# Second attention of a fused kernel: stacked f16 scores, projections spread between scores, unnormalized transposes, a swap by DMA

## What is computed

```python
q, k = rope(q, k)          # q*cos + rotate_half(q)*sin, likewise k
scores = einsum('bhqd,bhkd->bhqk', q, k) / sqrt(32)
tmp_attn = softmax(scores + causal)
tmp_sum = sum(tmp_attn, axis=-2)
topk_idx = top_k(tmp_sum, 25)        # "heavy" columns, per head
mask = heavy_mask | (abs(i - j) <= 25)
probs = softmax(where(mask, scores, lowest))
x = x + (einsum('bhqk,bhkd->bhqd', probs, v) -> (b, s, 512)) @ Wo.T
```

## Time and profile before

| | |
|---|---|
| median of 3 runs | 2003.69 us (2002.29 to 2006.08) |
| the profiled execution's own time | 2005.3 us |
| its span in the trace | 2003.5 us |
| TensorE (PE) busy | 1884.2 us, 94% of the span |
| VectorE (DVE), ScalarE (ACT), GpSimd (POOL) busy | 1347.1, 980.5, 127.0 us |
| second attention's first scores to next stage's first product | 72.88 to 719.71 us |

### The profile page before, as it was taken

How to read it: one execution, slowest core, us unless ns; L and a number is a source line. 1 busy time by engine, 2 the same in 40 slices (tenths; PEclk the granted TensorE clock), 3 DMA queues, 4 the chain that set the end, 5 groups by cost and what they waited for, 6 DMA issues and landing times.

```text
span 2003.5 us, 80904 instructions
## 1 busy us (share of the span) xinstructions
PE 1884.2 (94%) x34632; PEld 1646.3 (82%) x34632; DVE 1347.1 (67%) x5146; ACT 980.5 (49%) x3438; POOL 127.0 (6%) x213
## 2 busy tenths in 40 slices
PE   5899999899998889998899999999999999999998
PEld 3676776776777669998799899899998998998988
DVE  4476866767677665555767766767767777667664
ACT  2344653455435555665444554544554554545443
POOL 1120120210202101111000000000000000000000
PEclk9999999999999899999999999999999999999999
DMA  7011010110102113433000000100101000000000
GB/s 279 31 46 45 1 46 1 46 46 1 46 17 93 64 32 97 144 124 123 4 19 19 14 19 19 30 4 19 30 4 30 20 19 14 19 19 14 4 13 12
DMA packets 55611, 81.59 MB, mean 41 GB/s; under 512 B 5641, under 2 KB 42377, under 8 KB 54737
## 3 DMA queue, kind: packets, MB, share of 16 engines
q1 hardware_dynamic: 50960, 64.84, 9.7%
q0 software_dynamic: 4288, 11.55, 1.9%
HBM read 61.13 MB, written 15.24 MB: 38 GB/s over the span
## 4 chain that ended last, share of the span: by engine, by line
PE 53%; DVE 6%; ACT 2%; issue 1%; DMA 1%; DVEq 0%; ACTq 0%; POOLq 0%
PE ps L1348 27%; PE ps L1302 11%; PE ps L1281 10%; PE ps L1269 5%; DVE dh L1565 1%; ACT nn L1422 1%; DVE dh L1571 1%; DVE hn L1558 1%; DVE nxt L1574 0%; PE ps L1335 0%; DVE nxt L1577 0%; DVE tn L1540 0%; PE ps L1249 0%; DVE rn L1552 0%; DMA shared<-in_w2T 0%
## 5 line engine op out<-in xcount | busy, mean ns | idle before, releaser
L1348 PEld LDWEIGHTS ps<-nxt,whp 128*128 128x128 f16 x24576 | 649.2, 96 | 46.6 <-DVE nxt L1577 38.9
L1348 PE MATMUL ps<-nxt,whp 128*128 128x32 f16 x24576 | 655.8, 176 | 29.4 <-DVE nxt L1577 26.9
L1422 ACT ACTIVATE rz<-s,sc 128x32 f32<-128x32 f32 x512 | 164.8, 322 | 450.1 <-DVE s L1540 449.8
L1281 PE MATMUL ps<-cur,w1p 128*128 128x256 f16 x2112 | 271.8, 274 | 0.2 <-DVE wip L1716 0.2
L1302 PE MATMUL ps<-shared 128*128 128x256 f16 x2112 | 265.8, 273 | 0.0
L1302 PEld LDWEIGHTS ps<-shared 128*128 128x128 f16 x2112 | 205.6, 98 | 23.6
L1540 DVE TENSOR_REDUCE s<-ps 128x32 f32<-128x64 f32 x512 | 114.9, 224 | 162.5 <-PE ps L1348 161.6
L1281 PEld LDWEIGHTS ps<-cur,w1p 128*128 128x128 f16 x2112 | 198.3, 98 | 22.6 <-DVE wip L1716 0.4
L543 PE MATMUL ps<-kz,rot 128*128 128x256 f32 x512 | 156.5, 388 | 0.0
L1398 ACT ACTIVATE ps<-gi,sc 128x64 f32<-128x64 f32 x512 | 152.9, 299 | 0.1
L674 ACT ACTIVATE E<-ps,nm 128x128 f32<-128x128 f32 x256 | 94.4, 369 | 84.6 <-DVE nm L744 80.0
(11 more groups left out here) (216 smaller groups left out, 2898.8 us busy)
## 6 DMA issues: line engine op xcount, KB each, us to landing
gi<-gi_d SPq DMA_DIRECT2D x14, 768.0 KB, 5.0
seen<-in_w1T SPq DMA_DIRECT2D x8, 704.0 KB, 4.0
seen<-in_w2T SPq DMA_DIRECT2D x8, 704.0 KB, 5.3
gi_d<-shared SPq DMA_DIRECT2D x42, 128.0 KB, 1.9
gi_d<-b SPq DMA_DIRECT2D x42, 128.0 KB, 2.0
shared<-in_w1T POOLq DMA_DIRECT2D x20, 256.0 KB, 3.0
xall<-in_x SPq DMA_DIRECT2D x4, 1024.0 KB, 8.7
x1T<-in_xT SPq DMA_DIRECT2D x1, 4096.0 KB, 21.6
```

The source lines that it names most:

```text
L1281: last = nc.tensor.matmul(ps[:, 6 + n % 2, 0:TT], w1p[:, k, wp, i * P:(i + 1) * P], cur[:, k, hq, :, :].rearrange("p s b -> p (s b)"), sta ...
L1348: last = nc.tensor.matmul(ps[:, bank, g * WIDE * 2 * B:(g + 1) * WIDE * 2 * B], whp[:, k, w, q, g * P:(g + 1) * P], h, start=False, stop=( ...
L1422: nc.scalar.activation(o.rearrange("p g b -> p (g b)"), i_.rearrange("p g b -> p (g b)"), func, scale=scale).then_inc(done, 1)
```

## The change

The program of `second_attention` is rewritten on every engine.

- q and k are scaled by a power of two from their bounds, split into an f16 high part (ScalarE, `high`) and an f16 rest (VectorE, `low`), and laid out by DMA so that the 128 partitions of one head's operand hold its 32 rows four times: high, low, high, low for q against high, high, low, low for k (`stack`, 64 transfers a batch in two groups). One f16 product of 128x128 and one of 128x256 a head take the place of the f32 ones; `kz` goes. ScalarE's exponential gets a `scale` operand, and VectorE a multiplication of the maxima by it. VectorE takes maxima of two heads in one instruction.
- The partner rows of the rotation come by DMA: eight transfers of 16 partitions each for q and as many for k (`swap`).
- The next batch's 32 projection products and the last batch's 16 output products stand between the scores of the first pass, three a head. Copies, rotation, `high` and `low` stand between the heads on ScalarE and VectorE; v is projected while VectorE chooses columns.
- E is transposed without normalization; products of `rl` (reciprocal sums, broadcast) with the identity put the factors beside the values in PSUM, and VectorE multiplies four heads at a time (`normalize`).
- `rdiag`'s and `rl`'s reciprocals are taken for four heads at once; the weights' maxima stand in the second pass, in halves; weights of a batch are loaded in one go.
- Before the first batch VectorE takes maxima of hT, wq and wk for the scale, and scales the tables.

```diff
+                def swap(b, i):
+                    sp.wait_ge(a_raw, b * 4 + 2 * i + 2)
+                    if b:
+                        sp.wait_ge(v_rot, (b - 1) * 6 + 3 * i + 3)
+                    for c in range(8):
+                        to, fro = c * 16, (c ^ 1) * 16
+                        sp.dma_start(swp[to:to + 16, i, :, :], raw[fro:fro + 16, i, :, :]).then_inc(d_sw[i], 16)
...
+                def stack(b, group):
+                    if group == 0:
+                        sp.wait_ge(a_hi, 2 * (b + 1))
+                        sp.wait_ge(v_lo, 2 * (b + 1))
+                    if b:
+                        sp.wait_ge(p_s, (b - 1) * 2 * NH + NH + (group + 1) * NH // 2)
+                    for i, parts in enumerate(((0, 1, 0, 1), (0, 0, 1, 1))):
+                        for q in range(HPC):
+                            for j, part in enumerate(parts):
+                                h0 = group * NH // 2 + q
+                                sp.dma_start(stk[j * DH2:(j + 1) * DH2, i, h0:h0 + HPC + 1:HPC, :],
+                                             hl[q * DH2:(q + 1) * DH2, i, part, 2 * group:2 * group + 2, :])\
+                                    .then_inc(d_stk[group], 16)
...
+                for i in range(2):
+                    swap(0, i)
+                for group in range(2):
+                    stack(0, group)
...
+                    see(b)
+                    if b < B - 1:
+                        for i in range(2):
+                            swap(b + 1, i)
+                        for group in range(2):
+                            stack(b + 1, group)
+                sp.wait_ge(p_v, 2 * B)
...
-                    nc.tensor.matmul(ps[:, bank, 0:P], rot[:, 0, m, 0:P], kz[:, q, m, 0:P],
+                    nc.tensor.matmul(ps[:, bank, 0:P], stk[:, 0, h, 0:P], stk[:, 1, h, 0:P],
                                      start=False, stop=True, skip_group_check=True)
-                    nc.tensor.matmul(ps[:, bank, P:P + S], rot[:, 0, m, P:S], kz[:, q, m, :],
+                    nc.tensor.matmul(ps[:, bank, P:P + S], stk[:, 0, h, P:S], stk[:, 1, h, :],
                                      start=False, stop=True, skip_group_check=True).then_inc(p_s, 1)
...
+                def project(b, n):
+                    i, m, k = n // 16, n // 4 % 4, n % 4
...
+                    last = nc.tensor.matmul(ps[:, (4, 5, 6, 4)[n // 8], (m % 2) * S:(m % 2 + 1) * S],
+                                            (wq, wk)[i][:, k, m * P:(m + 1) * P], hT[:, k, b, :],
+                                            start=(k == 0 and m % 2 == 0), stop=(k == KD - 1), skip_group_check=True)
+                    if n % 8 == 7:
                         last.then_inc(p_qk, 1)
...
+                        last = nc.tensor.transpose(ps[:, (6, 4)[g % 2], c * P:(c + 1) * P],
+                                                   E[:, g % NEX, c * P:(c + 1) * P], ident)
...
+                    pe.wait_ge(v_rl, b * KD + m + 1)
+                    for q in range(HPC):
+                        for c in range(KS):
+                            last = nc.tensor.matmul(
+                                ps[q * DH2:(q + 1) * DH2, bank, S + c * P:S + (c + 1) * P],
+                                rl[:, m * HPC + q, c:c + 1].broadcast_to((P, DH2)), ident,
+                                start=False, stop=True, tile_position=(0, q * DH2), skip_group_check=True)
+                    last.then_inc(p_av, 1)
...
+                    beside = [(output, b - 1, n) for n in range(16)] if b else []
+                    beside = ([(project, b + 1, n) for n in range(32)] if b < B - 1 else []) + beside
+                    for h in range(NH + SUMS_BEHIND):
...
+                            for f, bb, n in beside[h * len(beside) // NH:(h + 1) * len(beside) // NH]:
+                                f(bb, n)
...
-                        project(b + 1)
-                    pe.wait_ge(v_k, b * K_STEPS + K_STEPS)
+                            column_sums(b, g // CGS)
                     for c in range(KS):
-                        last = nc.tensor.matmul(ps[:, 5, c * P:(c + 1) * P], light[:, c * P:(c + 1) * P],
+                        values_in(b, c)
+                    pe.wait_ge(v_k, (b + 1) * K_STEPS)
...
+                    for c, (e0, e1) in enumerate(((0, P), (P, P + S))):
+                        nc.scalar.activation(E[:, h % NEX, e0:e1], ps[:, bank_of(h), e0:e1], ACT.Exp,
+                                             bias=nm[:, r, h, c:c + 1], scale=sq[:, U:U + 1],
+                                             accum_out=ls[:, r, h, c:c + 1]).then_inc(a_e, 1)
+                def copy_raw(b, n):
+                    act.wait_ge(p_qk, b * 4 + n + 1)
...
+                def high(b, i):
+                    act.wait_ge(v_rot, b * 6 + 3 * i + 3)
...
+                                copy_raw(b + 1, RAW_AT.index(h))
+                            if h == HIGH_Q_AT:
+                                high(b + 1, 0)
+                    if b < B - 1:
+                        high(b + 1, 1)
+                    for c in range(KS):
...
+                    nc.vector.tensor_reduce(nraw[:, par, :, 0], ps[:, bank:bank + 2, 0:P], AX.X, ALU.max, negate=True)
+                    nc.vector.tensor_reduce(nraw[:, par, :, 1], ps[:, bank:bank + 2, P:P + S], AX.X, ALU.max,
+                                            negate=True).then_inc(v_mm, 1)
+                    dve.wait_ge(v_mm, n // 2 + 1)
+                    nc.vector.tensor_scalar(nm[:, r, h:h + 2, :], nraw[:, par, :, :], sq[:, U:U + 1], None, ALU.mult)\
+                        .then_inc(v_m, 1)
...
+                    if part == 0:
+                        dve.wait_ge(d_sw[i], 16 * 8 * (b + 1))
+                        tt(raw[:, i, :, :], raw[:, i, :, :], cos, ALU.mult).then_inc(v_rot, 1)
+                    if part == 1:
+                        tt(swp[:, i, :, :], swp[:, i, :, :], sin, ALU.mult).then_inc(v_rot, 1)
                         dve.wait_ge(v_rot, b * 6 + 3 * i + 2)
...
+                        tt(raw[:, i, :, :], raw[:, i, :, :], swp[:, i, :, :], ALU.add).then_inc(v_rot, 1)
+                def low(b, i):
+                    dve.wait_ge(a_hi, 2 * b + i + 1)
+                    dve.wait_ge(v_rot, b * 6 + 3 * i + 3)
+                    tt(hl[:, i, 1, :, :], raw[:, i, :, :], hl[:, i, 0, :, :], ALU.subtract).then_inc(v_lo, 1)
+                def sums_ready(b, j):
+                    dve.wait_ge(a_e, (b * 2 * NH + (j + 1) * CGS) * 2)
...
+                    nc.vector.reciprocal(rdiag[:, j * CGS:(j + 1) * CGS, :, j], ls[:, 0, j * CGS:(j + 1) * CGS, :])\
...
+                def normalize(b, m):
+                    dve.wait_ge(a_o, b * KD + m + 1)
+                    tt(oT[:, m, :], ps[:, (5, 7)[m % 2], S:2 * S], oT[:, m, :], ALU.mult).then_inc(v_o, 1)
...
+                step(nc.vector.memset(mh[:, :, :], 0.0))
+                for j in range(4):
+                    maximum(mh[:, 0, j:j + 1], shared[:, HT_AT + j * 2 * KD * S:HT_AT + (j + 1) * 2 * KD * S])
+                dve.wait_ge(d_w, 64)
+                dve.wait_ge(d_tab, 16)
+                maximum(mh[:, 1, 0:1], shared[:, 0:KD * D])
+                maximum(mh[:, 2, 0:1], shared[:, KD * D:2 * KD * D]).then_inc(v_init, 1)
+                dve.wait_ge(v_init, 1)
...
+                dve.wait_ge(p_sc, 1)
+                step(nc.vector.tensor_reduce(m3[:, :], ps[0:3, 7, 0:P], AX.X, ALU.max))
+                step(nc.vector.tensor_scalar(dg3[:, :], ident[0:3, 0:3], m3[:, 0:1], None, ALU.mult))
...
+                for i, c in enumerate((C_COSQ, C_COSK)):
+                    step(nc.vector.tensor_scalar(tab[:, c:c + 2 * S], tab[:, c:c + 2 * S], sq[:, 5 + i:6 + i], None,
+                                                 ALU.mult))
+                for i in range(2):
+                    rotate(0, i, 0)
+                    rotate(0, i, 1)
+                    low(0, i)
+                for b in range(B):
+                    for p in range(NH // 2):
+                        maxima(b, 0, 2 * p)
+                        if p % 2 == 0 and p >= 2:
+                            sums_ready(b, p // 2 - 1)
+                        if b < B - 1:
+                            if p == ROT_Q_AT:
+                                rotate(b + 1, 0, 0)
+                            if p == ROT_Q_AT + 1:
+                                rotate(b + 1, 0, 1)
+                            if p == ROT_K_AT:
+                                low(b + 1, 0)
+                                rotate(b + 1, 1, 0)
+                            if p == ROT_K_AT + 1:
+                                rotate(b + 1, 1, 1)
+                    if b:
+                        add(b - 1, 0)
+                    sums_ready(b, NH // CGS - 1)
+                    if b:
+                        add(b - 1, 1)
+                    heavy(b)
+                    columns(b)
...
+                    for p in range(NH // 2):
+                        maxima(b, 1, 2 * p)
```

(57 more changed lines are left out.)

513 lines of the change are left out of this document (248 added, 265 removed).

## The result

The changed kernel takes 2138.24 us (median of 4 runs, 2136.94 to 2142.11), the kernel before 2004.62 (median of 4, 2002.29 to 2006.08): 1.067 times as long, 95% interval 1.065 to 1.069. I had forecast 1975.5, faster. The profiled execution has a span of 2137.7 us.

The account below looks back on a forecast made before the run. TensorE was taken as the bound, busy 76.43 of a batch's 81.90 us. Start +16.9, batch 0's clock +1, seven batches -5.7 each and last batch -6.2 gave -28.2 us: 1975.5 from 2003.69, range 1915 to 2010.

Parts of the forecast that it names:

- I take 0.36 and 2.0: Transfers between SBUF partitions: 0.36 us an issue and 2.0 us to landing, taken from stores and loads.
- the stacks hide: Stack copies, two groups of 11.5 us of SP each, run behind the second pass and the next first pass.
- transfers in turn: Rival: each stack transfer holds its engines 2.0 us, so 64 take 128 us a batch; about 2340 us; chance 0.02.
- Start: Before the first batch: maxima, table scalings, rotation and 32 stack transfers put first scores at 89.8 us, 16.9 later.
- Batch: One full cycle: first pass and column choice 46.5 us, second pass 29.5, together 76.0, 5.7 less than 81.7.
- Last batch: Eighth batch, without projections: 68.5 us, 6.2 less than 74.7.
- the f16 scores' rate: TensorE's scores: 0.17 us a head in place of 0.71, saving 17 us a batch.
- the stall before the last column sum: First pass: TensorE idles 7 us until VectorE's chain of swaps, rotations and maxima gives the last reciprocals.
- No VectorE chain: Rival: VectorE's chain doesn't hold, the first pass is TensorE's 29 us, 9.5 us a batch less; 1909 us; chance 0.25.
- Swaps late: Rival: q's and k's swaps land at the stores' 5.4 us, 6.8 us a batch more; 2030 us; chance 0.14.
- Clock in the second pass: Rival: TensorE at half rate needs 2.2 us a head against ScalarE's 1.43, 11.7 a batch; 2069 us; chance 0.07.
- TensorE waiting for the stacks: Sign named in advance that the forecast is wrong: TensorE held up by the stack copies; no size given.

Follow-up runs that it names:

- e1: The changed kernel with nine sets of 16 transfers added on SyncE's queue at the end of the second attention; 2225.5 us against 2138.2.
- e4: The changed kernel with stacks by way of DRAM, two stores and 16 loads a batch in place of 64 copies; 2041.2 us, 85.7 a batch.
- e2: The changed kernel with half the stack copied from the second batch on, 32 transfers in place of 64 (scores wrong); 2063.7 us, 85.5 a batch.
- e9: e4 without the scaling: no maxima before the first batch, scale operand or multiplication of the maxima; 1983.5 us, 78.5 a batch.
- e6: e4 with room for eight heads of transposed E in place of four; 2035.0 us, 84.1 a batch.
- e5: e4 with the first half of v's projection moved ahead of the last column sum; 2025.2 us, 83.2 a batch.
- four edits: Those of e5, e6 and e9, and the next batch's k rotated by GpSimd; together on e4 1935.1 us, on the changed kernel's 64 copies 2068.1.

## Why the prediction was wrong

The step that failed is the price of a transfer: "I take 0.36 and 2.0", and on it "the stacks hide", with "11.5 us of SP each". What the runs showed in its place is 0.67 us an issue: 42.6 us of SyncE's queue a batch where I had 23. I had carried both ends of the landing into a rival, but the issue had only 0.36 or, in the rival of transfers in turn, the whole 2.0; nothing stood between them, though 80 issues a batch hang on it. The nearest rows were stores to DRAM and small loads from it; e1 shows that a copy inside SBUF is another kind. The rows were misread as well: the 0.32 of rows 9 is how long one instruction lasts, not how far apart two start. In the kernel before, two of these stores back to back last 0.80, so they start 0.48 apart, and so do the loads just ahead of those of rows 10:

```profile
47.65 0.43 SPq L453 DMA_DIRECT2D gb<-in_bias  x1
48.13 0.44 SPq L454 DMA_DIRECT2D bgi<-in_b_ih  x1
48.61 0.44 SPq L455 DMA_DIRECT2D bgi<-in_b_hh  x1
...
771.05 0.80 SPq L1204 DMA_DIRECT2D gi_d<-shared  x2
```

At 0.48 the 64 copies would take 31 us, which by the estimate of 0.52 above does not set the batch; so a right reading alone would not have been enough, and the rest had to be measured. The landing was right (1.9). My own sentence, that without the cover each us of a late stack delays a whole batch by one, then held for what went beyond the slack: 19.6 us more of issues cost some 10 a batch. The rule of the Trainium skill that I weighed (DMA: Bandwidth & Descriptors, Rules for kernel authors) pointed the right way, yet the transfers in turn at 2.0 us each that I made of it were wrong too: the queue overlaps landings (1.9 us), and the issues add. The section Anatomy of one DMA of that page, from which I had the 2 us, is on the path of GpSimd's issues, not of SyncE's.

Term by term, measured less forecast:

- Start: first scores 26.4 us later, forecast 16.9, so 9.5 late. The copies start at 76.98 (forecast 76.3), and 32 x (0.66 - 0.36) is 9.6.
- Batch: 95.7 against 76.0, 19.7 each and 138 in all. About 10 is the queue (it goes in e4, and in e2). Some 5 is the first pass: swaps cost 0.62 an issue and land 2.4 after it, so that eight take 7.4 in place of 4.9, first q's and then k's, with the chain behind them as forecast. Some 4 is the second pass: prices of ScalarE's instructions were right (0.46 and 0.57 for 0.45 and 0.55), but I had left out that ScalarE waits for VectorE's multiplication (e9) and for the values' room (e6): 7.0 us for four heads in place of 5.7.
- Last batch: 87.9 against 68.5, again with a wait for a stack, 12.25 us.

9.5 + 138 + 19.4 less the 1 us for batch 0's clock is 166 us; with 3 less in later stages, the 163 between 1975.5 and 2138.

What held: the f16 scores' rate (0.17 us a head); the stall before the last column sum and that VectorE's chain makes it; the low clock behind it, with v ending after the choice (e5); 85.7 us once the queue is out of the way is the forecast batch with its terms mis-sized by 9.7. "No VectorE chain" fell with the 75 us of waits for `rdiag`. "Swaps late" was right in direction, and its 6.8 us a batch stand near the some 5 measured by luck: it let each swap land after 5.4 us, while they landed after 2.4 and it is the issues that were slow. "Clock in the second pass" happened only in part: in the batch shown the granted clock was 1.00 from 351.60 to 385.80, but over three of the seven second passes it was 0.88 to 0.90, and these (from the chosen columns to the next first score, less its wait for a stack) took 34.8 to 35.9 us where the other four took 32.7 to 33.7. So it goes with 1 to 3 us in some batches, not with the 11.7 in each that I gave (16 x (2.2 - 1.43) would be 12.3). Of the signs of being wrong that I had named, "TensorE waiting for the stacks" is the one that came.

## What to carry to other kernels

When a change turns one engine's work into many transfers, count the issues in one in-order queue, give their price both ends as one does with the landing, and close the loop: what stands behind them in that queue and what feeds them again. Take that price from start to start, not from how long one instruction lasts (0.48 against 0.32 here), and measure it with the very ends and shapes of the copy, since even a store's full price was 0.2 us too low. Fix the queue first: four edits worth 14.7 us a batch kept 9.0 of it while the queue was full.

## What the hardware showed that I had not expected

SyncE's issue of a copy within SBUF takes 0.63 to 0.67 us from start to start at 32, 64 and 128 KB, over 16, 32 or 128 partitions, in runs of 512 bytes, 1 or 4 KB; with DRAM at one end 0.46 to 0.48, save a load of 32 partitions in two runs of 512 bytes (0.64); the loads of e4, 32 partitions in four runs of 1 KB, took 0.49 where nothing held them up. Why the one stands apart is open. GpSimd issued the same copies within SBUF every 0.54 us.
